# Expert results of a mixture-of-experts tower, added into the output by scatters: spare rows in place of a bound check

## Chip, cores and metric

One NeuronCore of one Trainium2 chip. The metric is the device time in microseconds, the median over runs of the whole kernel.

## The reference

Eight sequences of 512 tokens (4096 tokens, width 192) go through three layers. Each token's embedding comes from a small circuit simulation of angles looked up by token id; then one attention layer is added; then a mixture of experts:

```python
h = _L0_tok_ref(x, quantum_params, post_w, post_b)
h = h + _L0_attn_ref(_layernorm(h), W_qkv, b_qkv)
h = h + _L0_ffn_ref(_layernorm(h), Wg, W1, b1, W2, b2)
# _L0_ffn_ref: 8 experts, hidden width 384, two experts for each token
topk_scores, topk_idx = jax.lax.top_k(gate_scores, 2)
topk_probs = jax.nn.softmax(topk_scores, axis=-1)
hid = gelu(x @ W1[e] + b1[e]); y = hid @ W2[e] + b2[e]
out = sum over the two of topk_probs * y
```

So there are 8192 selections of an expert by a token, and each output row is the sum of a residual and two expert results.

## The kernel before, in words

The first part (up to about 190 us) gathers the angles (L472, GpSimd, 32 indirect DMAs), simulates the circuit on VectorE and GpSimd, runs the attention batch by batch, and stores the residual rows of each batch to `out` (`store`, SyncE). For each batch it also ranks the tokens within their two experts and scatters a short row of 32 numbers for every selection into the DRAM tensor `routed` (L657, 64 indirect DMAs of 128 rows of 128 bytes). Such a row has the token's compressed features, its gate share in column `SHARE` and its row number in `out` in column `DEST`. `routed` has one region for each expert; all of it is filled beforehand from `pad_rows` (L404, L406), whose `DEST` is `TOKENS` = 4096, one past the last row of `out`, and whose other columns are zero. So behind the tokens of an expert come pads, up to a whole block of 128.

The second part is the expert loop. It is unrolled over `BLOCKS` = 2 x 4096 / 128 + 8 - 1 = 71 blocks of 128 rows; what an expert's last block doesn't fill is pads, and blocks that no expert needs are pads alone. `block_table` (VectorE) works out, for each block m, its first row in `routed`, its expert's offset and, in `t_i[:, 1, m]`, how many blocks have to have landed in `out` before this one may be added: two blocks in flight must not hold the same token, since additions into the same row would lose one. Each engine has its own list for the loop, and they meet in semaphores:

- SyncE loads block m + 16 into a ring `xb` of 4 x 4 blocks when block m has been added (`added`, L446), and counts the blocks that landed in `landed`.
- TensorE, for each step of four blocks: `block_transpose` (L1944), `up_proj` (L1962), `pick_up` (L1951); and for each block `down_proj` (L1972), into one of the two banks of `bank_b`, when `y_done` shows that block m - 2 has been read.
- ScalarE: the Gelu (L1651) and copies.
- VectorE: `weighted(m)` (L1473) waits for `y_mm` (the matmul of block m) and, from m = 8 on, for the landing of block m - 8 (`added`), multiplies the result by the share column into one of `RESULTS` = 8 buffers `y`, and signals `y_done`. Once in four blocks it also makes a mask (`expert_of`, L1418).
- GpSimd: for each block it reads the count of `t_i` (L705), waits for `y_done` and for `landed`, and issues the scatter of 128 rows of 768 bytes with addition (L709), indexed by the `DEST` column of `xb`, with `bounds_check=TOKENS - 1`: rows whose index is greater (the pads) are dropped.

`constants` (GpSimd, L663 on) makes index tables with iota, early in the kernel, ahead of `last_string` (L500 on).

Of the kernel before, what the change touches and what calls it, by code (L numbers as in the profile page):

```python
# [8 lines left out]
ALU = mybir.AluOpType  # L9
ACT = mybir.ActivationFunctionType  # L10
AX = mybir.AxisListType
F32 = mybir.dt.float32
I32 = mybir.dt.int32
# [18 lines left out]
def build(nc, token_ids, angles, emb_two, emb_raw, qkv_w, gate_w, up_w, down_w, out):  # L32

    P = 128
    TOKENS = token_ids.shape[0] * token_ids.shape[1]
    BATCHES, SEQ = token_ids.shape
# [3 lines left out]
    TILES = SEQ // P  # L40
# [6 lines left out]
    STEP = 4  # L47
# [3 lines left out]
    RING = 4  # L51
    SEEN = BATCHES - 2
    RESULTS = 8
# [19 lines left out]
    SHARE, DEST = UNIT + 1, UNIT + 2  # L73
# [1 line left out]

    routed = nc.dram_tensor("routed", (ROWS, F), F32, kind="Internal").ap()
    ids_view = token_ids.rearrange("b (p j) -> p b j", j=TILES)
    out_rows = out.rearrange("b s d -> (b s) d")
    out_view = out.rearrange("b (p j) d -> b p (j d)", j=TILES)

    ctx = ExitStack()
    with ctx:  # L82
        def sb(name, shape, dt=F32):
            return ctx.enter_context(nc.sbuf_tensor(name, shape, dt))

        def sem(name):
            return ctx.enter_context(nc.semaphore(name))
# [49 lines left out]
        pad_rows = sb("pad_rows", [P, REGION // P, F])  # L137
# [38 lines left out]
        def behind(room, pattern, **sizes):  # L176
            size = int(np.prod(list(sizes.values())))
            room[1] += size
            return room[0][:, room[1] - size:room[1]].rearrange(pattern, **sizes)
# [49 lines left out]
        whole = sb("whole", [P, 1])  # L229
        steps_late = sb("steps_late", [P, RING])  # L230
        need = sb("need", [P, RING], I32)
        seen = sb("seen", [P, 2, E])
        shared_last = sb("shared_last", [P, 3, E - 1])
        first_late = sb("first_late", [P, E - 1])
# [7 lines left out]
        xb = behind(up_room_1, "p (r n f) -> p r n f", r=RING, n=STEP, f=F)  # L242
        y = behind(up_room_1, "p (n d) -> p n d", n=RESULTS, d=D)
# [16 lines left out]
        pads_ready = sem("pads_ready")  # L260
# [88 lines left out]
        added = [sem(f"added{n}") for n in range(RESULTS)]  # L349
# [33 lines left out]
        def hold(eng):  # L383

            eng.sem_inc(passed, 1)  # L385
# [66 lines left out]
        def _(pool):  # L452
            steps = [0]

            def step(instruction):
                steps[0] += 1
                instruction.then_inc(pool_step, 1)

            def join():
                pool.wait_ge(pool_step, steps[0])  # L460
# [201 lines left out]
            def constants():  # L662
                step(pool.iota(blk_i[:, :], [[1, BLOCKS]], base=0, channel_multiplier=0))  # L663
                step(pool.iota(exp_i[:, :], [[1, E]], base=0, channel_multiplier=0))
                pool.wait_ge(ones_done, 1)
                step(pool.affine_select(out=before_f[:, :], in_=ones[:, :], compare_op=ALU.is_gt, fill=0.0, base=0,
                                        pattern=[[1, P]], channel_multiplier=-1))
                pool.wait_ge(rows_clear, 1)
                step(pool.memset(rows[:, :, :, :, UNIT:UNIT + 1], 1.0))
                for k in range(2):  # L670
                    step(pool.iota(rows[:, :, k, :, DEST].bitcast(I32), [[SEQ, BATCHES], [1, TILES]], base=0,
                                   channel_multiplier=TILES))
                join()
                step(pool.tensor_copy(blk[:, :], blk_i[:, :]))
                step(pool.tensor_copy(exp_f[:, :], exp_i[:, :]))
                step(pool.tensor_copy(before[:, :], before_f[:, :]))
                join()
                pool.sem_inc(const_done, 1)

            gather_angles(COUNT[0], COUNT[0] + GATHERS_EARLY)  # L680
            join()
            constants()
            last_string(0)
            gather_angles(COUNT[0] + GATHERS_EARLY, ANGLE_LAST[1])
# [19 lines left out]
            for m in range(BLOCKS):  # L704
                last_shared = pool.value_load(t_i[0:1, 1, m:m + 1], min_val=1, max_val=BLOCKS + 1)  # L705
                pool.wait_ge(y_done, m + 1)
                pool.wait_ge(landed, last_shared)
                hold(pool)
                pool.indirect_dma_start(  # L709
                    out=out_rows, out_offset=bass.IndirectOffsetOnAxis(  # L710
                        xb[:, m // STEP % RING, m % STEP, DEST:DEST + 1].bitcast(I32), 0),
                    in_=y[:, m % RESULTS, :], in_offset=None, bounds_check=TOKENS - 1,
                    oob_is_err=False, compute_op=ALU.add).then_inc(added[m % RESULTS], 16)

        @block.vector
        def _(dve):
            steps = [0]

            def step(instruction):
                steps[0] += 1  # L720
                instruction.then_inc(dve_step, 1)

            def join():
                dve.wait_ge(dve_step, steps[0])
# [322 lines left out]
            step(dve.memset(u_rep[:, :, :, :, :], 0.0))  # L1047
            step(dve.memset(w_rep[:, :, :, :, :], 0.0))
            join()
            dve.memset(pad_rows[:, :, DEST:DEST + 1].bitcast(I32), TOKENS).then_inc(pads_ready, 2)  # L1050

            dve.wait_ge(lifted_done, 1)
            dve.tensor_copy(lqk0[:, :, :], bank_a[:, 0:2, 0:P])
# [415 lines left out]
            def weighted(m):  # L1469
                dve.wait_ge(y_mm, m + 1)  # L1470
                if m >= RESULTS:
                    dve.wait_ge(added[m % RESULTS], 16 * (m // RESULTS))
                dve.tensor_scalar(y[:, m % RESULTS, :], bank_b[:, m % 2, 0:D],  # L1473
                                  xb[:, m // STEP % RING, m % STEP, SHARE:SHARE + 1], None, ALU.mult).then_inc(y_done, 1)

            for m in range(BLOCKS):
                weighted(m)
                if m % STEP == 1 and m // STEP + 2 < STEPS:
                    expert_of(m // STEP + 2)
# [563 lines left out]
```

## Time and profile before

| | |
|---|---|
| median of three runs | 338.76 us (336.81 to 340.1) |
| span of the profiled execution | 338.6 us |
| busy share POOL / PE / PEld / DVE / ACT | 74% / 71% / 48% / 52% / 28% |
| expert loop, first to last scatter | 194.5 to 332.0 us |

The profiled execution is one run under the hardware profiler; its time is the span, from the first to the last instruction. POOL is GpSimd, PE TensorE's matmuls, PEld its weight loads, DVE VectorE, ACT ScalarE, SP SyncE; an engine's name with q is its sequencer. For an indirect DMA, the busy time of POOL is what the engine spends on the instruction, and "landing" is when the data has arrived. A row's "idle before" names what the engine's idle time ended with.

### The profile page before, as it was taken

How to read it: one execution, taken by the hardware profiler on the slowest of the kernel's cores; microseconds unless marked ns; L12 is line 12 of the kernel's file. 1: busy time of each engine (PE TensorE's matmuls, PEld its weight loads, DVE VectorE, ACT ScalarE, POOL GpSimd, SP SyncE). 2: the span in 40 equal slices, each digit the busy share in tenths (PEclk: the TensorE clock that was granted, in tenths of full speed). 3: DMA queues.
4: the chain of work that ended last, by engine and by line, in shares of the span. 5: the costliest groups of instructions: out<-in, count | busy, mean ns of one | idle time of the engine just before them, and what ended most of it. 6: DMA issues, size and time to landing. Idle time of an engine off the chain costs nothing. (4 is left out here: it accounts for less than half of the span.)

```text
span 338.6 us, 6221 instructions
## 1 busy us (share of the span) xinstructions
PE 240.9 (71%) x1585; PEld 162.0 (48%) x1585; DVE 177.6 (52%) x698; ACT 95.2 (28%) x223; POOL 250.2 (74%) x283
## 2 busy tenths in 40 slices
PE   0831973668478989768654899999999587999500
PEld 0621641223243445444421678777777365877400
DVE  5758997488998866684699322232222122122200
ACT  1002001354324144634233323332432132133000
POOL 5778979309968777766777388888883888888673
PEclk9999995558955556965555599999999799699955
DMA  6710019900000001111123146656461556564510
GB/s 191 201 13 11 0 45 400 382 5 2 2 0 9 12 13 60 63 57 60 59 70 103 22 54 69 64 62 67 53 69 18 60 62 65 61 69 50 59 10 0
DMA packets 28141, 22.61 MB, mean 67 GB/s; under 512 B 15434, under 2 KB 25546, under 8 KB 27787
## 3 DMA queue, kind: packets, MB, share of 16 engines
q0 software_dynamic: 13296, 7.95, 21.1%
q1 hardware_dynamic: 14524, 14.23, 13.0%
q8 instruction: 15, 0.25, 0.3%
q14 instruction: 18, 0.15, 0.2%
q10 hardware_dynamic: 288, 0.03, 0.1%
HBM read 7.25 MB, written 15.63 MB: 68 GB/s over the span
## 5 line engine op out<-in xcount | busy, mean ns | idle before, releaser
L709 POOL DMA_INDIRECT out<-up x71 | 110.3, 1554 | 33.1 <-issue 13.9
L1972 PE MATMUL bank_b<-down,up 128*128 x426 | 91.2, 354 | 5.0 <-DVE up L1473 1.0
L1972 PEld LDWEIGHTS bank_b<-down,up 128*128 128x128 f32 x426 | 72.9, 200 | 22.6 <-issue 18.8
L1473 DVE TENSOR_SCALAR up<-bank_b,up 128x192 f32<-128x192 f32 x71 | 29.6, 418 | 97.5 <-PE bank_b L1972 84.9
L657 POOL DMA_INDIRECT routed<-rows,slot x64 | 61.9, 968 | 23.9 <-issue 18.0
L472 POOL DMA_INDIRECT theta_all<-angles,ids x32 | 32.4, 1012 | 10.9 <-issue 9.0
L1651 ACT ACTIVATE up<-bank_a 128x384 f32<-128x384 f32 x71 | 31.3, 497 | 3.4 <-PE bank_a L1962 2.9
L1775 PE MATMUL bank_b<-queries_t,keys_t 32*128 32x512 f32 x64 | 26.1, 900 | 6.9 <-ACT keys_t L1499 3.4
L1782 PE MATMUL bank_a<-keys_t,wt 32*128 32x512 f32 x64 | 27.6, 949 | 3.8 <-DVE nmax L1133 2.1
L1663 ACT COPY up<-bank_c 128x384 f32<-128x384 f32 x18 | 8.6, 478 | 61.8 <-PE bank_c L1951 58.7
L1133 DVE TENSOR_REDUCE nmax<-bank_a 128x2 f32<-128x1024 f32 x16 | 19.5, 1219 | 11.5 <-PE bank_a L1782 11.3
L1521 ACT ACTIVATE prob<-bank_b 128x1024 f32<-128x1024 f32 x16 | 16.4, 1023 | 18.2 <-PE bank_b L1775 18.2
L1951 PE MATMUL bank_c<-up_all,up 128*128 128x384 f32 x36 | 16.6, 545 | 6.6 <-DVE up L1418 4.4
L1962 PE MATMUL bank_a<-up 32*128 32x128 f32 x426 | 18.5, 304 | 0.6 <-ACT up L1657 0.5
L1962 PEld LDWEIGHTS bank_a<-up 32*128 32x128 f32 x426 | 15.1, 201 | 5.6 <-issue 4.5
L1848 PE MATMUL bank_a<-m,a2t 32*128 32x192 f32 x64 | 14.3, 536 | 4.8 <-ACT hres L1529 2.7
L1848 PEld LDWEIGHTS bank_a<-m,a2t 32*128 32x128 f32 x64 | 7.7, 277 | 11.9 <-issue 10.6
L1794 PE MATMUL bank_c<-prob,u 128*32 128x128 f32 x256 | 12.6, 361 | 0.8 <-ACT prob L1521 0.7
L1657 ACT COPY up<-bank_d 128x128 f32<-128x128 f32 x18 | 4.8, 266 | 25.3 <-PE bank_d L1944 25.3
L1775 PEld LDWEIGHTS bank_b<-queries_t,keys_t 32*128 32x128 f32 x64 | 7.1, 255 | 9.9 <-issue 8.6
L1794 PEld LDWEIGHTS bank_c<-prob,u 128*32 128x32 f32 x256 | 9.3, 145 | 5.0 <-ACT prob L1521 2.3
L1951 PEld LDWEIGHTS bank_c<-up_all,up 128*128 128x128 f32 x36 | 6.9, 212 | 8.5 <-issue 3.3
(420 smaller groups left out, 369.4 us busy)
## 6 DMA issues: line engine op xcount, KB each, us to landing
routed<-pad_rows SPq DMA_DIRECT2D x8, 528.0 KB, 5.7
out<-hres SPq DMA_DIRECT2D x8, 384.0 KB, 2.4
down<-down_w SPq DMA_DIRECT2D x1, 2304.0 KB, 11.9
up<-up_w SPq DMA_DIRECT2D x1, 1536.0 KB
out<-up POOLq DMA_INDIRECT x71, 3.5
up<-routed SPq DMA_DIRECT2D x69, 16.0 KB
routed<-rows,slot POOLq DMA_INDIRECT x64
up<-up_w SPq DMA_DIRECT2D x1, 780.0 KB
```

What stands on the lines that cost most here:

```text
L472: pool.indirect_dma_start(out=theta_all[:, t, :], out_offset=None, in_=angles, in_offset=bass.IndirectOffsetOnAxis(ids[:, b, j:j + 1], 0)) ...
L657: pool.indirect_dma_start(out=routed, out_offset=bass.IndirectOffsetOnAxis(slot[:, b, k, j:j + 1], 0), in_=rows[:, b, k, j, :], in_offset=None
L709: pool.indirect_dma_start(out=out_rows, out_offset=bass.IndirectOffsetOnAxis(xb[:, m // STEP % RING, m % STEP, DEST:DEST + 1].bitcast(I32) ...
L1473: dve.tensor_scalar(y[:, m % RESULTS, :], bank_b[:, m % 2, 0:D], xb[:, m // STEP % RING, m % STEP, SHARE:SHARE + 1], None, ALU.mult).then_ ...
L1651: act.activation(hid[:, n, :], bank_a[:, n, 0:HID], ACT.Gelu).then_inc(gelu_done, 1)
L1775: mm = pe.matmul(bank_b[:, n, :], keys_t[r, bt % 3, k * P:(k + 1) * P], queries_t[r, :], start=True, stop=True)
L1782: mm = pe.matmul(bank_a[:, n, :], wt[r, bs % 2, :], keys_t[r, bs % 3, :], start=True, stop=True)
L1794: mm = pe.matmul(bank_c[j * F:(j + 1) * F, 0:P], u[:, b * TILES + k, :], prob[:, k, j * P:(j + 1) * P], start=(k == 0), stop=(k == TILES - 1),
L1848: mm = pe.matmul(bank_a[:, 2 + n, 0:D], a2t[r, :], m2[r, :], start=True, stop=True)
L1951: pe.matmul(bank_c[:, 0:HID], pick[:, s % 2].rearrange("p n f -> p (n f)"), up_all[:, :], start=True, stop=True).then_inc(picked, 1)
L1962: mm = pe.matmul(bank_a[:, n, c * P:(c + 1) * P], up_now[r, s % 2, c * P:(c + 1) * P], xt[r, 0, :], start=True, stop=True)
L1972: mm = pe.matmul(bank_b[:, m % 2, 0:D], hid[:, m % STEP, c * P:(c + 1) * P], down[:, bass.ds(first + c * D, D)], start=(c == 0), stop=(c = ...
```

## The change

The output in DRAM gets 8 x 128 spare rows behind the 4096 of the tokens, which are cut off at the end. GpSimd makes a table `spare` of their numbers (column n: rows 4096 + 128 n + partition). Pads get a `DEST` beyond all of them. In `weighted(m)` VectorE takes the minimum of the block's `DEST` column and the spare column m % 8, into `target`; a token's row number stays, a pad gets a spare row of its own. The scatter is indexed by `target` and has no bound check, so that all 128 rows of each block are added somewhere.

```diff
-    out_rows = out.rearrange("b s d -> (b s) d")
-    out_view = out.rearrange("b (p j) d -> b p (j d)", j=TILES)
+    out_view = out[0:TOKENS, :].rearrange("(b p j) d -> b p (j d)", b=BATCHES, j=TILES)
...
+        spare = sb("spare", [P, RESULTS], I32)
+        target = sb("target", [P, RESULTS], I32)
...
                 step(pool.iota(exp_i[:, :], [[1, E]], base=0, channel_multiplier=0))
+                step(pool.iota(spare[:, :], [[P, RESULTS]], base=TOKENS, channel_multiplier=1))
...
                 pool.indirect_dma_start(
-                    out=out_rows, out_offset=bass.IndirectOffsetOnAxis(
-                        xb[:, m // STEP % RING, m % STEP, DEST:DEST + 1].bitcast(I32), 0),
-                    in_=y[:, m % RESULTS, :], in_offset=None, bounds_check=TOKENS - 1,
-                    oob_is_err=False, compute_op=ALU.add).then_inc(added[m % RESULTS], 16)
+                    out=out, out_offset=bass.IndirectOffsetOnAxis(target[:, m % RESULTS:m % RESULTS + 1], 0),
+                    in_=y[:, m % RESULTS, :], in_offset=None, compute_op=ALU.add).then_inc(added[m % RESULTS], 16)
...
-            dve.memset(pad_rows[:, :, DEST:DEST + 1].bitcast(I32), TOKENS).then_inc(pads_ready, 2)
+            dve.memset(pad_rows[:, :, DEST:DEST + 1].bitcast(I32), TOKENS + RESULTS * P).then_inc(pads_ready, 2)
...
                     dve.wait_ge(added[m % RESULTS], 16 * (m // RESULTS))
+                dve.tensor_tensor(target[:, m % RESULTS:m % RESULTS + 1],
+                                  xb[:, m // STEP % RING, m % STEP, DEST:DEST + 1].bitcast(I32),
+                                  spare[:, m % RESULTS:m % RESULTS + 1], ALU.min)
                 dve.tensor_scalar(y[:, m % RESULTS, :], bank_b[:, m % 2, 0:D],
...
-    out = nc.dram_tensor("out", (x.shape[0], x.shape[1], embed), F32, kind="ExternalOutput").ap()
+    out = nc.dram_tensor("out", (x.size + 8 * 128, embed), F32, kind="ExternalOutput").ap()
```

## Rows read from the trace of the kernel before

**Rows 1.** Page, part 5: the costliest group of instructions (busy, mean ns, idle before).

```profile
L709 POOL DMA_INDIRECT out<-up x71 | 110.3, 1554 | 33.1 <-issue 13.9
```

**Rows 2.** Busy time in two stretches: PE, PEld, DVE, ACT, POOL, clock, DMA, GB/s.

```profile
194.00:254.00 60.00, 58.39 (x474) 46.95 (x476) 17.05 (x46) 21.02 (x55) 49.69 (x32) 0.99 0.57 62
254.00:294.00 40.00, 32.41 (x235) 25.56 (x228) 8.20 (x23) 9.18 (x24) 29.58 (x20) 0.87 0.48 53
```

**Rows 3.** Timeline of POOL in the expert loop: start, us, what, idle before it.

```profile
194.46 1.62 POOL L709 DMA_INDIRECT out<-up  x1 [4.30 <-DVE up L1473]
196.57 1.58 POOL L709 DMA_INDIRECT out<-up  x1 [0.50 <-issue]
...
246.97 1.55 POOL L709 DMA_INDIRECT out<-up  x1 [0.30 <-SPq L446]
...
252.54 1.55 POOL L709 DMA_INDIRECT out<-up  x1 [0.30 <-issue]
256.87 1.55 POOL L709 DMA_INDIRECT out<-up  x1 [2.77 <-issue]
260.78 1.55 POOL L709 DMA_INDIRECT out<-up  x1 [2.36 <-DVE up L1473]
...
318.33 1.55 POOL L709 DMA_INDIRECT out<-up  x1 [0.30 <-issue]
...
322.71 1.55 POOL L709 DMA_INDIRECT out<-up  x1 [2.83 <-issue]
...
332.01 1.56 POOL L709 DMA_INDIRECT out<-up  x1 [0.30 <-issue]
```

**Rows 4.** Timeline of DVE in the expert loop: start, us, what, idle before.

```profile
195.26 0.42 DVE L1473 TENSOR_SCALAR up<-bank_b,up 128x192 f32<-128x192 f32 x1 [1.74 <-PE bank_b L1972]
...
244.55 0.42 DVE L1473 TENSOR_SCALAR up<-bank_b,up 128x192 f32<-128x192 f32 x1 [1.20 <-PE bank_b L1972]
...
247.14 0.42 DVE L1473 TENSOR_SCALAR up<-bank_b,up 128x192 f32<-128x192 f32 x1 [0.87 <-PE bank_b L1972]
247.47 0.28 DVE L1418 TENSOR_TENSOR up<-feature,up 128x128 f32<-128x128 f32 x1
...
253.77 0.42 DVE L1473 TENSOR_SCALAR up<-bank_b,up 128x192 f32<-128x192 f32 x1 [0.98 <-PE bank_b L1972]
...
259.82 0.42 DVE L1473 TENSOR_SCALAR up<-bank_b,up 128x192 f32<-128x192 f32 x1 [1.89 <-DMA out<-up]
...
311.13 0.42 DVE L1473 TENSOR_SCALAR up<-bank_b,up 128x192 f32<-128x192 f32 x1 [0.87 <-PE bank_b L1972]
...
318.26 0.42 DVE L1473 TENSOR_SCALAR up<-bank_b,up 128x192 f32<-128x192 f32 x1 [0.72 <-PE bank_b L1972]
```

**Rows 5.** L709, L657, L472, each by its line: ns min/median/max; landing of L709.

```profile
L709 POOL DMA_INDIRECT out<-up x71: 1550/1552/1619, 194.5 to 332.0; - x71
...
DMA to landing us min/median/max: 2.7/3.5/5.0
...
L657 POOL DMA_INDIRECT routed<-rows,slot x64: 952/958/1255, 100.8 to 189.2; - x64
...
L472 POOL DMA_INDIRECT theta_all<-angles,ids x32: 947/952/1707, 3.4 to 62.6; - x32
```

**Rows 6.** DVE's groups by line and shape: a small two-input operation.

```profile
L1277 DVE TENSOR_TENSOR gap<-gap,rs 128x4 f32<-128x4 f32 x8 | 1.3, 159 | 0.1
```

**Rows 7.** L709 by its line, 316 to 334 us alone: landing.

```profile
DMA to landing us min/median/max: 2.7/2.7/3.5
```

**Rows 8.** Timelines of DVE and POOL early in the kernel: start, us, what.

```profile
50.28 0.98 DVE L1098 TENSOR_TENSOR form_p<-ev,form_w 128x784 f32<-128x784 f32 x1
...
29.34 0.16 POOL L664 IOTA exp_i<- 128x8 int32 x1
...
31.79 0.49 POOL L500 TENSOR_TENSOR last_r<-turn 128x144 f32<-128x144 f32 x1 [0.83 <-DVE tails L812]
...
50.38 1.71 POOL L472 DMA_INDIRECT theta_all<-angles,ids  x1 [0.30 <-issue]
```

More of the change, by code:

```diff
@@ L2038 @@
                                   kind="ExternalInput").ap())
-    out = nc.dram_tensor("out", (x.shape[0], x.shape[1], embed), F32, kind="ExternalOutput").ap()
+    out = nc.dram_tensor("out", (x.size + 8 * 128, embed), F32, kind="ExternalOutput").ap()
     build(nc, *aps, out)
     result = run_bass_kernel_spmd(nc, [arrays], core_ids=[0])
-    return result.results[0]["out"]
+    return result.results[0]["out"][0:x.size].reshape(x.shape[0], x.shape[1], embed)
```

## The prediction

> **What bounds the kernel now.** The page's busy shares come first: GpSimd (POOL) is the busiest engine (the table above). A share of the whole span proves nothing, so the costliest groups come next: the largest is the 71 accumulating scatters of L709, 110.3 us [rows 1]. Then the stretches of the expert loop: from 194 to 254 us POOL is busy 49.7 of 60 us, PE 58.4 [rows 2]. Which of the two sets the pace is read from the timelines, where both engines' rows stand in order of m. On POOL m=0 starts at 194.46, and in the steady part a scatter takes 1.55 us with 0.30 us of issue before it, 1.856 us a block [rows 3]. On DVE the results of m=1 and m=37 start at 195.26 and 253.77: 58.5 us over 36 blocks, 1.625 us a block; this is PE's own pace, since DVE waits there for PE alone [rows 4]. POOL is slower by 0.23 us a block, and falls behind.
>
> That is visible in the middle. POOL starts m=31 at 252.54, m=32 at 256.87 and m=33 at 260.78, 4.33 and 3.91 apart [rows 3], though m=33's result was begun at 247.14 [rows 4]. These are waits for `landed`. The reference's own inputs tell why. Worked out from them, five experts take 3251, 735, 4, 4096 and 106 of the 8192 selections and three take none, so 26, 6, 1, 32 and 1 blocks, and behind them five blocks of nothing but pads (m=66 to 70). The table that L705 reads makes m=32 wait for m=31 to land, m=33 for m=32, m=65 for m=64. The third gap is 318.33 to 322.71, 4.38 us [rows 3]. With POOL already late, the first two gaps use up the ring of eight results: DVE waits for a scatter to land before m=40 [rows 4], PE starves, and its granted clock is 0.87 from 254 to 294 us, against 0.99 before [rows 2]. The last result starts at 318.26 [rows 4], but the last scatter only at 332.01, 6.6 us before the end. So the loop's end is POOL's: 70 steps of 1.856, and 4.33 + 3.91 + 4.38 - 3 x 1.856 = 7.05 for the gaps, and 0.5 for two slow first steps, from 194.46, give 331.9; read: 332.01 [rows 3]. What one scatter costs POOL is the term that decides.
>
> **The change, part by part.** (a) The scatter without bound check. No row shows an accumulating one without it. The nearest rows are the same engine's two other indirect DMAs, also of 128 rows each, without a check: the scatter L657 has a median of 958 ns, the gather L472 952 ns, L709 1552 ns [rows 5]. L709 differs from them in three things: check, addition, and row length (768 bytes against 128 and 144). Between the two short ones length changes nothing, and moved data isn't the cause: the blocks of pads move nothing, yet their scatter at 332.01 takes 1.56 us as well [rows 3]. What is left is the check or the addition, or both. Ends: 0.96 (all the excess is the check's) and 1.55 (none is), and nothing excludes a small rise above 1.55. I take 0.96: a dropped row costs POOL as much as a kept one, which looks like a test of each index, while an addition that needs work for each row would have had nothing to do for dropped ones. That is an inference, and weighs perhaps two to one.
>
> The Trainium skill (DMA: Bandwidth & Descriptors, "SWDGE vs HWDGE vs iDMA") states that one DMA operation is one read and one write descriptor. By that an addition adds none, which points to the check; but the same page ("SDMA does more than copy") calls the addition a reduction of two streams, and no row here shows how many descriptors that takes. By the first the sum is the one below, by the second the no-change case.
>
> At 0.96 + 0.30 = 1.26 us a block POOL is faster than PE's 1.625, so it follows PE. It starts 1.31 us behind DVE (195.26 to 196.57) [rows 3, 4], and 0.15 later with (b). m=31's result starts at 244.55 [rows 4]; POOL then starts m=31 at 246.0. The three waits stay, but shorten by what the scatter shortens, 0.59: m=32 at 246.0 + 4.33 - 0.59 = 249.75; m=33 at 249.75 + 3.91 - 0.59 + 0.5 = 253.6 (0.5: m=32 has 124 pads, now real writes). That is 5.0 us behind 247.14 + 1.46; POOL wins back 0.37 us a block and has caught up by m=47. The ring isn't reached: m=41's result is due at 260.3, m=33 has landed by about 257.2. So PE keeps 1.625: m=65's result starts at 253.77 + 28 x 1.625 = 299.3, m=64's 1.3 earlier (PE's shorter steps), at 298.0. POOL starts m=64 at 299.5, m=65 at 299.5 + 4.38 - 0.59 = 303.3, m=70 at 303.3 + 5 x 1.26 = 309.6. DVE's last result, 299.3 + 7.1 (311.13 to 318.26 now [rows 4]) = 306.4, is earlier. So late next are the last wait for landing and five scatters of pads behind it.
>
> (b) An integer minimum of 128x1 on DVE before each multiplication. Nearest row: a two-input operation on 128x4, 159 ns [rows 6]; the ends are 0 and the 0.28 us of L1418 on 128x128 [rows 4]; I take 0.15. DVE is busy 17.05 of 60 us [rows 2], so its own time is hidden. It delays y_done. Behind that wait POOL's scatter (the 0.15 above) and PE's down_proj(m+2), which has two banks: one multiplication takes 0.42, and in the fastest stretch, m=65 to m=70, results are 1.43 us apart (311.13 to 318.26), so some 0.8 of cover stays. Without it the price is 71 x 0.15 = 10.6 us.
>
> (c) Pads are now moved: 71 x 128 - 8192 = 896 rows of 768 bytes. The 16 DMA engines are held 0.57 of 194 to 254 us for 32 scatters and their loads [rows 2]: 1.07 us a block, under 1.26. Landing has a median of 3.5 us overall [rows 5], but 2.7 in the last stretch, where the rows are dropped [rows 7]: the last one comes 0.8 later. From 0 to 2 us; I take 0.8, beside the 0.5 above.
>
> (d) One more iota of 128x8 in `constants`: L664, of that size, takes 0.16 us, and POOL then idles 0.83 us for DVE before L500 [rows 8]. Nothing; uncovered it would be 0.16. The other memset constant and the output's shape change no duration.
>
> **The sum.** Last scatter at 309.6; from its start to the end it is 338.6 - 332.01 = 6.6 now, less 0.59, plus 0.8: 6.8. New span 316.4 against 338.6: 22.2 less. The profiled execution's span, 338.6, is 0.2 below the median of the three runs, 338.76 (336.81 to 340.1); 338.8 - 22.2 = 316.6.
>
> **The rivals.** No change: the excess belongs to the addition, and L709 stays at 1.55. The same chain holds, with 0.15 + 0.5 + 0.8 for (b) and (c): 340.2. For it: no row separates addition from check. Against: dropped rows at full price.
>
> Shared: check and addition take half each, L709 at 1.25. POOL's pace is 1.55, still under PE's. m=33 starts at 254.2, 5.6 late; by m=64 it wins back 31 x 0.075 = 2.3: m=64 at 302.8, m=65 at 306.9, m=70 at 314.6, the end at 321.7, so 321.9.
>
> Slower: the minimum on DVE holds POOL up while it writes a scatter. If POOL stands still for all of it and gains nothing by the check, its pace is 1.856 + 0.15: 340.2 + 70 x 0.15 = 350.7. It passes 1% once each scatter grows by (3.4 - 1.45) / 70 = 28 ns. For: at 50.28 a two-input DVE operation of 0.98 us runs, and the gather of 50.38 takes 1.71 instead of 0.95 [rows 8]. Against: one of 0.28 us at 247.47 lies inside the scatter of 246.97, which still takes 1.55 [rows 3, 4]. The Trainium skill (GPSIMD Engine Reference, "Key points") says that GpSimd shares its SBUF interfaces with VectorE and contends with operations of two SBUF inputs; the pair at 50 us agrees, the one at 247 us doesn't.
>
> **How the numbers follow.** The whole excess removed 0.57 (316.6, its own range 313 to 320), shared 0.10 (321.9), no change 0.26 (340.2), slower 0.07 (350.7). About 1% is what a measurement of this kernel can tell from no change. Faster by over 1%: 0.57 + 0.10 = 0.67; within: 0.26; slower: 0.07. The range goes from 313 (the likeliest case with a shorter tail and a PE a little quicker) to 341, over the no-change case, without which a third would be left out.
>
> **What would show it.** L709 at 0.95 to 1.0 us with 0.30 before it; its starts 1.4 to 1.5 behind DVE's up to m=31; gaps of 3.6 to 3.8 at m=32, m=33 and m=65; no DVE wait for a scatter; PE's clock near 1.0 until its last block; DVE's last result at 306 to 307; a new DVE operation of about 0.15 us; last landings of about 3 us. If L709 still reads 1.55, step (a) is wrong. If it reads 0.96 but the end lies above 320, the waits for landing have grown, and (c) is wrong.

## The result, and the profile after

The changed kernel takes 340.18 us (median of 20 runs, 338.33 to 341.98), the kernel before 338.81 us (20 runs): ratio 1.0041, interval 1.0022 to 1.006. So it is 1.4 us slower (by the interval 0.7 to 2.0), where 22 us less were forecast. The prediction was wrong, and it was wrong at the first row to read. Two groups of the page of the kernel after (line, engine, operation, count; busy, mean ns; idle before):

```profile
L711 POOL DMA_INDIRECT out<-up,target x71 | 110.4, 1554 | 32.7 <-SPq L447 12.8
...
L1473 DVE TENSOR_TENSOR target<-up,spare 128x1 int32<-128x1 int32 x71 | 11.3, 160 | 93.4 <-PE bank_b L1975 79.3
```

The scatter without bound check costs GpSimd 1554 ns, as with it [rows 1]. The minimum on VectorE is there, 160 ns. The timeline of POOL in the kernel after stands beside [rows 3], for m=0, then m=31, 32 and 33, m=64 and 65, and m=70, the last one:

```profile
193.13 1.62 POOL L711 DMA_INDIRECT out<-up,target  x1 [3.20 <-DVE up L1476]
...
251.34 1.55 POOL L711 DMA_INDIRECT out<-up,target  x1 [0.30 <-issue]
255.63 1.55 POOL L711 DMA_INDIRECT out<-up,target  x1 [2.74 <-issue]
260.14 1.55 POOL L711 DMA_INDIRECT out<-up,target  x1 [2.96 <-DVE up L1476]
...
317.72 1.55 POOL L711 DMA_INDIRECT out<-up,target  x1 [0.31 <-issue]
322.10 1.55 POOL L711 DMA_INDIRECT out<-up,target  x1 [2.83 <-issue]
...
331.40 1.56 POOL L711 DMA_INDIRECT out<-up,target  x1 [0.30 <-issue]
```

From the first start to the last it is 331.40 - 193.13 = 138.27 us; before it was 332.01 - 194.46 = 137.55. Of these 0.72 us, 0.60 lie in one place, the step from m=32 to m=33: 4.51 us, before 3.91. The steps to m=32 (4.29) and to m=65 (4.38) are about those of before (4.33 and 4.38). From the last start to the end of the span of 338.8 it is 7.4 us, before 6.6. Together that is 1.5 us, which agrees with the 1.4 us of the medians. The two spans differ by only 0.2, because in the profiled execution of after the first scatter happened to start 1.3 us earlier (193.13 against 194.46).

VectorE still waits for a landing before m=40, as in [rows 4], and in the stretch of 254 to 294 us PE is busy 32.7 us, before 32.4, POOL 29.9, before 29.6 [rows 2]. DVE's row, and the stretch (columns as in [rows 2]):

```profile
259.25 0.16 DVE L1473 TENSOR_TENSOR target<-up,spare 128x1 int32<-128x1 int32 x1 [2.29 <-DMA out<-up,target]
```

```profile
254.00:294.00 40.00, 32.74 (x230) 25.48 (x229) 10.06 (x42) 11.49 (x30) 29.92 (x20) 0.96 0.50 55
```

PE's granted clock in this stretch is 0.96, before 0.87. In all the traces here with an addition in each scatter the stretch reads 0.87 to 0.91 without the minimum on VectorE (five traces) and 0.91 to 0.96 with it (four). Why is open. It brings no time, because POOL sets the pace there.

What the pads do in the DMA queue stands in part 3 of the page: GpSimd's queue with packets, MB and the share of the 16 DMA engines, for the kernel before, the kernel after, and the first experiment below (no addition).

```profile
q0 software_dynamic: 13296, 7.95, 21.1%
q0 software_dynamic: 13296, 8.63, 22.5%
q0 software_dynamic: 6480, 8.63, 9.2%
```

Moving the 896 pads adds 0.68 MB, which is 896 x 768 bytes, but not one packet: a dropped row has its packet too. Leaving the addition out takes away 6816 packets, 96 for each of the 71 scatters.

The landing in the last stretch, by the scatter's line from 316 us on, is now 3.5 us where [rows 7] read 2.7:

```profile
DMA to landing us min/median/max: 3.4/3.5/3.6
```

The end of the span has a row that the forecast had not looked at. The sequencer of POOL executes a DRAIN instruction at the end of the block of engine programs. By its line, first in the kernel before, then in the kernel after (duration in ns, then start in us):

```profile
L82 POOLq DRAIN  x1: 9841/9841/9841, 328.5 to 328.5; - x1
```

```profile
L81 POOLq DRAIN  x1: 10732/10732/10732, 327.8 to 327.8; - x1
```

The first ends at 338.3, the second at 338.5, and the span 0.3 later in both.

### The profile page after: what moved, and what is told of

It is laid out like the page before. It is cut to its first block and busy times, and to the rows that moved or that the text cites. A ratio compares the mean times of both kernels' runs of the same rounds, so it can differ in the third digit from the quotient of the medians.

```text
span 338.8 us, 6222 instructions
## 1 busy us (share of the span) xinstructions
PE 239.4 (71%) x1585; PEld 160.3 (47%) x1585; DVE 181.7 (54%) x769; ACT 95.4 (28%) x223; POOL 251.2 (74%) x284
## 3 DMA queue, kind: packets, MB, share of 16 engines
q0 software_dynamic: 13296, 8.63, 22.5%
## 5 line engine op out<-in xcount | busy, mean ns | idle before, releaser
L711 POOL DMA_INDIRECT out<-up,target x71 | 110.4, 1554 | 32.7 <-SPq L447 12.8
L1975 PE MATMUL bank_b<-down,up 128*128 x426 | 89.4, 349 | 5.9 <-issue 2.3
L1975 PEld LDWEIGHTS bank_b<-down,up 128*128 128x128 f32 x426 | 71.6, 196 | 22.9 <-issue 18.9
L658 POOL DMA_INDIRECT routed<-rows,slot x64 | 62.6, 977 | 23.0 <-issue 18.3
L1473 DVE TENSOR_TENSOR target<-up,spare 128x1 int32<-128x1 int32 x71 | 11.3, 160 | 93.4 <-PE bank_b L1975 79.3
```

Source lines behind the costliest of these rows:

```text
L658: pool.indirect_dma_start(out=routed, out_offset=bass.IndirectOffsetOnAxis(slot[:, b, k, j:j + 1], 0), in_=rows[:, b, k, j, :], in_offset=None
L711: pool.indirect_dma_start(out=out, out_offset=bass.IndirectOffsetOnAxis(target[:, m % RESULTS:m % RESULTS + 1], 0), in_=y[:, m % RESULTS, ...
L1975: mm = pe.matmul(bank_b[:, m % 2, 0:D], hid[:, m % STEP, c * P:(c + 1) * P], down[:, bass.ds(first + c * D, D)], start=(c == 0), stop=(c = ...
```

## The experiments

**Without addition, without check** (the expert scatter of after).

```diff
-    in_=y[:, m % RESULTS, :], in_offset=None, compute_op=ALU.add)
+    in_=y[:, m % RESULTS, :], in_offset=None)
```

> The kernel after without the addition: each scatter overwrites its rows, so the sum over the two experts and the residual is left out. Theory A (the 0.6 us that the expert scatter costs POOL over the other indirect DMAs belong to the addition): 0.96 us a scatter instead of 1.55, starts 1.26 us apart where POOL sets the pace and PE's 1.625 us else, and by the forecast's chain an end near 316.6 us, ratio 0.93 to before. Theory B (they belong to the row length, 768 bytes against 128 and 144): 1.55 us and 340.2 us, ratio 1.004.

Measured: 319.23 us, ratio 0.9424 (0.938 to 0.9468). Shown are the scatter's line (ns, landing), the timeline of POOL at m=31, 32, 33, 64, 65 and 70, the stretch from 254 to 294 us, and the drain:

```profile
L711 POOL DMA_INDIRECT out<-up,target x71: 954/959/967, 193.3 to 309.3; - x71
...
DMA to landing us min/median/max: 2.3/2.3/4.2
```

```profile
245.58 0.96 POOL L711 DMA_INDIRECT out<-up,target  x1 [0.66 <-SPq L447]
248.77 0.96 POOL L711 DMA_INDIRECT out<-up,target  x1 [2.23 <-SPq L447]
252.29 0.96 POOL L711 DMA_INDIRECT out<-up,target  x1 [2.56 <-DVE up L1476]
...
299.68 0.95 POOL L711 DMA_INDIRECT out<-up,target  x1 [0.41 <-issue]
302.82 0.96 POOL L711 DMA_INDIRECT out<-up,target  x1 [2.18 <-DVE up L1476]
...
309.33 0.96 POOL L711 DMA_INDIRECT out<-up,target  x1 [0.30 <-issue]
```

```profile
254.00:294.00 40.00, 38.35 (x322) 30.72 (x314) 13.56 (x56) 13.79 (x36) 25.46 (x27) 1.00 0.25 75
```

```profile
L81 POOLq DRAIN  x1: 8854/8854/8854, 308.6 to 308.6; - x1
```

Theory A holds and B falls: rows of 768 bytes cost 959 ns when they aren't added. The run also tests the rest of the forecast, whose condition it makes true: m=31 at 245.58 (forecast 246.0), m=33 at 252.29 (253.6), m=64 at 299.68 (299.5), m=65 at 302.82 (303.3), m=70 at 309.33 (309.6), PE's clock 1.00. Two things are off. The steps to m=32, 33 and 65 are 3.19, 3.52 and 3.14 us, where the forecast had 3.74, 3.82 and 3.79. The first and the last are 1.1 and 1.2 us shorter than before, as the landing is (2.3 against 3.5), and not by the 0.59 of the scatter. This doesn't show at m=64, because by then POOL only follows PE. So the run bears out the pace, and not the price of the waits. And the end is off: it comes 317.7 - 309.33 = 8.4 us behind the last start instead of 6.8. Its drain ends at 317.5, 5.9 us after the last landing (309.33 + 2.3). In the kernel before it is 338.3 - (332.01 + 2.7) = 3.6 us. Why the drain takes longer here wasn't tried.

**With check, without addition** (the kernel before, less its addition).

```diff
-    oob_is_err=False, compute_op=ALU.add)
+    oob_is_err=False)
```

> The kernel before, bound check kept, without the addition (the sum over experts is left out). Theory A: the check costs nothing beside the addition or alone, so 0.96 us a scatter, and about 1.4 us less than the run without check and without addition (no minimum on VectorE, no pads moved): some 315.2 us, ratio 0.93. Theory C (check and addition hide behind each other, each alone would cost 1.55): 1.55 us and no change, ratio 1.00. Theory B: 1.55 us too.

Measured: 318.18 us, ratio 0.9391 (0.9341 to 0.944). By the scatter's line:

```profile
L709 POOL DMA_INDIRECT out<-up x71: 982/983/996, 192.6 to 308.2; - x71
```

983 against 959 ns: without addition the kernel with the check has a scatter that costs 24 ns more (it also takes its index from `xb` and not from `target`). Theory C falls. The time is 3.0 us above the 315.2 expected: the end is again 8.4 us behind the last start (316.6 - 308.23), and the run is 1.05 us below the one without check, not 1.4.

**The minimum with pads dropped; and a check that drops nothing.** Both are the kernel after with a bound check put back. The first bound drops all pads, the second none:

```diff
+    bounds_check=TOKENS - 1, oob_is_err=False                  # one kernel
+    bounds_check=TOKENS + RESULTS * P - 1, oob_is_err=False    # the other
```

> The kernel after with the bound check of before (4095): the minimum on VectorE stays, pads are dropped again. Theory P (the 1.4 us lost come from moved pads): 0.15 us over before, ratio 1.0005, the gap between m=32 and m=33 back at 3.9 us and the last start 6.6 us before the end. Theory M (they come from the minimum, which delays every result): ratio 1.004 as the kernel after.

> The kernel after with a bound check that drops nothing (its bound is the last spare row). Both theories of the scatter's cost: 1.55 us, ratio 1.004 as the kernel after, gap between m=32 and m=33 at 4.5 us, last start 7.4 us before the end. If the check costs anything by itself, each scatter is longer than 1.554 us in the mean and the ratio above 1.004: 0.02 us a scatter would be 1.4 us, another 0.4%.

Measured: 337.98 us, ratio 0.998 (0.9951 to 1.0009), with pads dropped; 340.69 us, ratio 1.0051 (1.0021 to 1.0081), with a check that drops none. POOL's timeline at m=31, 32, 33 and 70, first pads dropped, then none dropped:

```profile
250.55 1.55 POOL L711 DMA_INDIRECT out<-up,target  x1 [0.30 <-issue]
254.78 1.55 POOL L711 DMA_INDIRECT out<-up,target  x1 [2.68 <-issue]
258.73 1.55 POOL L711 DMA_INDIRECT out<-up,target  x1 [2.40 <-DVE up L1477]
...
329.90 1.56 POOL L711 DMA_INDIRECT out<-up,target  x1 [0.30 <-issue]
```

```profile
251.95 1.55 POOL L711 DMA_INDIRECT out<-up,target  x1 [0.30 <-issue]
256.36 1.55 POOL L711 DMA_INDIRECT out<-up,target  x1 [2.85 <-issue]
260.79 1.55 POOL L711 DMA_INDIRECT out<-up,target  x1 [2.88 <-DVE up L1477]
...
332.08 1.56 POOL L711 DMA_INDIRECT out<-up,target  x1 [0.30 <-issue]
```

The two kernels differ in the bound's value alone. Step m=32 to 33: 3.95 against 4.43 us; last start to end of span: 336.4 - 329.9 = 6.5 against 339.3 - 332.08 = 7.2. So the loss is that of the moved pads (theory P), and the minimum costs nothing that these runs can tell (theory M falls). All traces with an addition in each scatter bear out the step to m=33: it reads 3.90 to 4.12 us in the six in which pads are dropped, and 4.43, 4.51 and 4.53 in the three in which they are moved. The step to m=32 is no such sign: it reads 4.23 to 4.94 with pads dropped. The medians of the two kernels are 2.7 us apart, more than the 1.2 of these two places; where the rest comes from isn't shown, but a part of the difference of the profiled spans, 1.1 us, lies ahead of the first scatter. The scatter's mean is 1554 and 1555 ns in them, 1554 without a check: beside an addition the check costs 1 ns at most.

**Nine forms in one kernel.** The kernel after, with the form of the scatter chosen by m modulo 9. It was executed once; only durations on POOL are read.

```diff
-    pool.indirect_dma_start(out=out, ... in_=y[:, q, :], compute_op=ALU.add)
+    if m % 9 == 0: ...    # rows, columns, add, check differ: one line of code each
```

> The kernel after with nine forms of the scatter in turn (block m uses form m modulo 9): with and without addition, with 128 or 64 rows, with 192, 128 or 32 columns (the narrow ones go to scratch tensors), with and without a check that drops nothing. Much of the output's sum is left out; only the durations on POOL count. Theory A1 (the addition costs POOL work for each row): 128 rows with addition 1.55 us at 192, 128 and 32 columns alike; without it 0.96 at all widths; 64 rows with addition longer than 64 rows without by half of 0.6, 0.30. Theory A2 (the addition costs a fixed amount per DMA): 64 rows longer by the full 0.6. Theory A3 (addition is dear only for rows over 512 bytes): 0.96 with addition at 128 and 32 columns. The check: 0.02 us without addition (983 against 959 ns in the two runs before), nothing with it.

The groups by line and shape (L715: 128 rows, 192 columns, added; L719: the same, plain; L723 and L727: 64 rows, added and plain; L731: 32 columns, added; L739 and L744: with check, added and plain; L749: 128 columns, added):

```profile
L731 POOL DMA_INDIRECT short<-up,target x8 | 12.7, 1590 | 2.5 <-issue 2.2 <-SPq L449 0.3
L715 POOL DMA_INDIRECT out<-up,target x8 | 12.6, 1571 | 5.3 <-DVE up L1514 3.8 <-issue 0.9 <-SPq L449 0.6
L739 POOL DMA_INDIRECT out<-up,target x8 | 12.5, 1567 | 4.9 <-DVE up L1514 2.4 <-SPq L449 1.3 <-issue 1.1
L723 POOL DMA_INDIRECT out<-up,target x8 | 11.5, 1443 | 5.3 <-issue 3.7 <-DVE up L1514 1.6
L749 POOL DMA_INDIRECT middle<-up,target x7 | 10.9, 1555 | 2.2 <-issue 2.2
L744 POOL DMA_INDIRECT out<-up,target x8 | 8.3, 1034 | 2.4 <-issue 1.8 <-DVE up L1514 0.3 <-SPq L449 0.3
L719 POOL DMA_INDIRECT out<-up,target x8 | 7.9, 991 | 2.6 <-issue 1.4 <-SPq L449 0.6 <-DVE up L1514 0.6
...
L727 POOL DMA_INDIRECT out<-up,target x8 | 7.4, 927 | 2.4 <-DVE up L1514 0.9 <-issue 0.9 <-SPq L449 0.6
```

The width changes little (added: 1590, 1555 and 1571 ns at 32, 128 and 192 columns; plain: 988 and 991 at 32 and 192), so A3 falls. Half the rows save 8%: 1443 ns for 64 rows. The addition's excess is 580 ns at 128 rows and 516 at 64: nearer to A2, a fixed amount for each DMA, than to A1. The check costs 43 ns here without addition (1034 against 991) and nothing with it (1567 against 1571). Means of seven or eight scatters in a mixed kernel are 17 to 32 ns above those of the kernels with one form (991 against 959, 1571 against 1554).

**Five row counts.** Ten forms in turn: 128, 96, 64, 32 and 16 rows, added and plain, again in one execution. Shown are 128 and 16 rows, added (L713, L745) and plain (L717, L749).

```diff
+    if m % 10 == 0: ... target[0:128] ... y[0:128, q, :], compute_op=ALU.add
+    elif m % 10 == 1: ... target[0:128] ... y[0:128, q, :]        # and so on down to 0:16
```

> The kernel after with ten forms of the scatter in turn (m modulo 10): 128, 96, 64, 32 and 16 rows, each with and without addition, 192 columns, no check. Much of the output's sum is left out; only durations count. Theory A2' (the addition costs POOL mostly a fixed amount): the excess with addition stays near 0.45 us down to 16 rows, as 0.58 at 128 and 0.52 at 64 rows in the run before suggest (0.45 + 128 x 0.001). Theory A1 (it costs for each row, but two groups of rows are worked on side by side, so that 64 rows show little less than 128): the excess falls below 0.2 us at 32 rows and to 0.1 at 16.

```profile
L713 POOL DMA_INDIRECT out<-up,target x8 | 12.8, 1596 | 7.4 <-SPq L447 3.4 <-DVE up L1514 3.1 <-issue 0.9
...
L745 POOL DMA_INDIRECT out<-up,target x7 | 9.2, 1318 | 2.9 <-SPq L447 1.9 <-issue 0.7 <-DVE up L1514 0.3
L717 POOL DMA_INDIRECT out<-up,target x7 | 6.9, 984 | 2.3 <-issue 1.4 <-DVE up L1514 0.9
...
L749 POOL DMA_INDIRECT out<-up,target x7 | 6.0, 857 | 2.1 <-issue 1.8 <-SPq L447 0.3
```

The excess is 612, 539, 529, 468 and 461 ns at 128, 96, 64, 32 and 16 rows: about 0.45 us for being an adding DMA, and between 16 and 128 rows 1.3 ns a row on average. A plain one costs 857 ns at 16 rows and 984 at 128. So A2' holds. What GpSimd does in the fixed part isn't shown. It isn't a wait for earlier scatters: m=32 and m=33 start when those before them have landed, and take 1.55 us like the others.

**No drain at the end** (the kernel before).

```diff
-    block = ctx.enter_context(nc.Block())
+    block = ctx.enter_context(nc.Block(no_gpsimd_drain=True))
```

> The kernel before, the block of engine programs left without GpSimd's drain at its end (all scatters' landings are waited for by SyncE as before). In the trace of before that drain ends at 338.3, 3.6 us after the last scatter's landing at about 334.7. Theory D (the end is the drain's): about 3.4 us less, ratio 0.990. Theory L (the end is the landing and the meeting of the engines): no change, ratio 1.000.

Measured: 335.88 us, ratio 0.9919 (0.9886 to 0.9952). The last start in POOL's timeline, in a span of 336.0:

```profile
332.70 1.56 POOL L709 DMA_INDIRECT out<-up  x1 [0.30 <-issue]
```

The last start is followed by 3.3 us instead of 6.6: the end was the drain's, theory D. The medians gained 2.6 us, by the interval 1.6 to 3.9, where 3.4 were expected. This also says how the pads cost 0.8 us at the end of the kernel after: they delay the landing (2.7 to 3.5), and with 71 adding scatters the drain ends 3.6 us after it, before and after.

**No scatter for blocks that no expert needs** (the kernel before). VectorE copies the number of blocks used into an integer tile `total`, and GpSimd and SyncE branch by it:

```diff
+    blocks_used = pool.value_load(total[0:1, 0:1], min_val=1, max_val=BLOCKS)
...
-    pool.indirect_dma_start(...)
+    if m < 2 * TOKENS // P: scatter_add()
+    else:
+        with pool.If(blocks_used > m): scatter_add()      # SyncE: the wait for it alike
```

> The kernel before, where GpSimd branches around the scatters of blocks that no expert needs (from m=64 on, by the number of blocks used, 66 here) and SyncE around their waits. The chain of POOL's scatters loses five of 1.856 us: 9.3 us less, a little back for five branches and a full landing (3.5 instead of 2.7 us): ratio 0.975. The rival, that the end is set by something beside POOL's chain (VectorE's last result at 318.3, PE): at least 5 us less are then still to be had, as the last result is 16 us before the end; a branch on GpSimd or SyncE that costs over a microsecond each would show as a gain under 5 us.

Measured: 331.37 us, ratio 0.9802 (0.9758 to 0.9845). POOL's last two starts (m=64, 65) and the drain:

```profile
316.57 1.55 POOL L719 DMA_INDIRECT out<-up  x1 [0.30 <-issue]
321.12 1.55 POOL L719 DMA_INDIRECT out<-up  x1 [2.99 <-issue]
```

```profile
L82 POOLq DRAIN  x1: 3953/3953/3953, 325.1 to 325.1; - x1
```

There are 66 scatters instead of 71. The last starts at 321.12, against 332.01 before, but the end is 8.1 us behind it, not 6.6: the drain runs to 329.1. Of these 1.5 us, 0.7 are the landing of a scatter with real rows (3.4 us instead of 2.7); for the rest the drain ends 4.5 us after the landing, not 3.6, and why stays open. The gain is 7 us, not the 8.5 expected. No rival holds, and the missing part is mostly at the end.

**Both.**

> Both edits on the kernel before: the branch around unneeded blocks and no drain of GpSimd at the end. If they are independent, the gains add: 9.3 - 1.0 + 3.4, about 11.7 us, ratio 0.965. If the drain only waits for what the last scatters leave, and the branch shortens that already, less than the sum.

Measured: 328.65 us, ratio 0.9711 (0.9664 to 0.9758). The last start, in a span of 326.6, and SyncE's arrival at the end of its program:

```profile
321.25 1.55 POOL L719 DMA_INDIRECT out<-up  x1 [3.08 <-issue]
```

```profile
L82 SPq COMPARE_BRANCH  x1: 38/38/38, 326.2 to 326.2; - x1
```

The sum of the two measured gains would be 1.98 + 0.81 = 2.8%; measured are 2.9%, where 3.5% were expected. So they add, each smaller than expected. 5.3 us follow on the last start, 3.3 without the branches: the landing takes 0.7 longer (real rows), and SyncE gets to the end at 326.2, 1.5 us after the landing at about 324.7 (321.25 + 3.4). In the kernel without drain and branches it was there 0.1 us after the landing. The five branches that SyncE has to go through are the likely reason; no run separates them. This version is the fastest of the kernels here that compute the whole output: 2.9% below the kernel before, and by the ratios 3.3% below the kernel after (0.9711 / 1.0041 = 0.967).

**The change on top of that version, and the version again beside it.**

> The whole change (spare rows, minimum, no check) on top of the version that branches around unneeded blocks and has no drain. Theory P (moved pads are what the change costs, through the landings that are waited for): the five blocks of pads are gone, and the last scatter, m=65, has 22 pads and moves its data in either version, so nothing is lost at the end; left is the wait between m=32 and m=33, 0.5 to 0.6 us longer: ratio 0.9711 + 0.002 = 0.973 at most. The rival (the change costs something per block or elsewhere): the full 1.4 us again, 0.975.

> The version that branches around unneeded blocks and leaves out the drain, once more, on the chip and in the rounds of the run with the change on top, so that the two can be set against each other: ratio 0.971 as before, gap between m=32 and m=33 at 3.9 us.

Measured: 329.59 us, 0.9729 (0.9697 to 0.9762), with the change; 328.14 us, 0.9708 (0.9664 to 0.9751), without. POOL at m=31, 32, 33, first with the change, then without:

```profile
250.18 1.55 POOL L721 DMA_INDIRECT out<-up,target  x1 [0.30 <-issue]
255.54 1.55 POOL L721 DMA_INDIRECT out<-up,target  x1 [3.81 <-issue]
260.07 1.55 POOL L721 DMA_INDIRECT out<-up,target  x1 [2.98 <-DVE up L1492]
```

```profile
250.60 1.55 POOL L719 DMA_INDIRECT out<-up  x1 [0.30 <-issue]
255.08 1.55 POOL L719 DMA_INDIRECT out<-up  x1 [2.92 <-issue]
259.07 1.55 POOL L719 DMA_INDIRECT out<-up  x1 [2.45 <-DVE up L1489]
```

The step to m=33 is 4.53 against 3.99 us, as theory P has it. But the medians are 1.45 apart, and the step to m=32, a wait for the landing of m=31, reads 5.36 against 4.48. The 33 pads of m=31 don't explain this: in the other pairs the step doesn't follow them (4.29 moved and 4.33 dropped; 4.41 and 4.23), and in the kernel before without its drain, where pads are dropped, it reads 4.94. Nor do pads explain the step to m=65 (4.97 against 4.63), as m=64, whose landing it waits for, has none. The intervals overlap, and the run doesn't decide between 0.6 and 1.4 us. That stays open.

## Why the prediction was wrong

- **What bounds the loop** was right: POOL's chain of scatters, one after another, with three waits for landings. Making the scatter 959 ns by leaving the addition out took the time from 338.99 to 319.23 us; the kernel with five scatters fewer gained 7 us.
- **Step (a) failed**: "I take 0.96". All the excess of L709 over the other indirect DMAs was put down to the check, and it is the addition's: the scatter without check takes 1554 ns. At 128 rows 959 of the 1554 ns are a plain scatter's and 595 the addition's; the check's share is 24 to 43 ns without the addition and about nothing beside it. The row that the forecast leaned on, equal cost for dropped and kept rows, was read as a sign of the check. It holds, but it shows something else. The argument "an addition that needs work for each row would have had nothing to do for dropped ones" fails twice. Most of the addition's cost is by the instruction, 461 ns at 16 rows already. And what is by the row isn't saved either: 16 rows cost 278 ns less than 128 (1318 against 1596), but a scatter whose 128 rows are all dropped costs as much as a full one (1.56 us). The packets fit this: dropped rows have theirs too (13296 in both kernels). That POOL does its work for dropped rows as for kept ones is what these figures suggest; it wasn't tried by itself. The rule of the Trainium skill (DMA: Bandwidth & Descriptors, "SWDGE vs HWDGE vs iDMA"), one read and one write descriptor for a DMA operation, was no guide to this: 112 rows more in one DMA (16 to 128) cost 127 ns plain, the addition 461 ns at 16 rows already. And an adding scatter isn't the same work for the queue: it has 96 packets more than a plain one.
- **The no-change case** was priced right, though it had a chance of only 0.26: 340.2 forecast, 340.18 measured. Its terms: 0.5 at m=33 (0.60 measured, 0.48 in the pair of bounds), 0.8 at the end (0.8, 0.7). The 0.15 for the minimum was too high: it takes 0.16, but the multiplication starts 0.08 behind its start, and the kernel with the minimum and pads dropped wasn't slower (0.998 of before, at most 1.0009). That the sum hits to 0.02 us is luck, as the interval of the difference is 1.3 us wide.
- **The chain** held in the run without addition, to 1.3 us at m=33 and 0.3 at m=70, the second in part because POOL had caught up with PE by m=64, so that the error of the first two waits (0.8 us together) was gone. Its tail was missed by 1.6, since "from its start to the end" was carried over without asking what fills it: the drain.
- **Slower, by contention with VectorE**: the scatter's mean is 1554 ns with 71 minimum operations in the kernel and without. In the trace of after 50 scatters have a whole minimum operation inside them and 13 none at all, and both take 1.55 us in the mean. The Trainium skill's warning (GPSIMD Engine Reference, "Key points") isn't seen at operations of 0.16 us.
- **Shared** (check and addition half each) fell at once with the 1554 ns without check, and again with the 983 ns with check and without addition.

## What to carry to other kernels

A price difference between two groups of instructions that differ in three attributes is a question, not a price: where no row separates them, likelihoods such as two to one are too bold for a forecast of 22 us. When GpSimd's indirect DMAs set the pace, count instructions first: fewer DMAs, or plain ones where the sum can be had elsewhere. The bound check and the number of rows in a DMA mattered little here. Whatever is sent to spare rows is moved for real, and is paid where a landing is waited for.

## What was not expected of the hardware

- An adding indirect DMA costs POOL 1318 ns at 16 rows and 1596 at 128; a plain one 857 and 984; columns hardly matter (32 to 192).
- A row that the bound check drops still has its DMA packet (13296 packets with 896 rows dropped or moved) and saves GpSimd no time; it only lands sooner (2.7 us against 3.5). An adding scatter has 96 packets more than a plain one.
- The bound check costs 24 to 43 ns a scatter of 128 rows without addition, 0 to 1 ns with it.
- The drain of GpSimd at the end of the program outlasts the last landing by 3.6 us in the kernel before, and leaving it out brings 2.6 us (338.48 to 335.88). In the run of plain scatters it outlasts the landing by 5.9 us, in the one with branches by 4.5; what sets that is open.
- A branch around a scatter costs little: in four timelines with it the step to m=65 is 4.55, 4.63, 4.64 and 4.97 us, in five without it 4.32 to 4.48.
